# A graph network's convolution loops: sixteen additions on VectorE become one scan over feature-major blocks, with the turning done by ScalarE

## The reference

```python
def gcn_conv(x, edge_index, W, b, num_nodes):
    src = concatenate([edge_index[0], arange(num_nodes)])
    dst = concatenate([edge_index[1], arange(num_nodes)])
    deg = segment_sum(ones_like(dst), dst)
    dinv = where(deg > 0, rsqrt(deg), 0.0)
    norm = dinv[src] * dinv[dst]
    h = x @ W
    return segment_sum(h[src] * norm[:, None], dst) + b

h = relu(gcn_conv(x, edge_index, W1, b1, n))
out = relu(gcn_conv(h, edge_index, W2, b2, n))
```

## Time and profile before

| what | value |
|---|---|
| median of the runs | 10099.72 us |
| span of the profiled execution | 11181.7 us |
| first convolution, first gather to last addition | 3850.1 to 6042.5 us |
| second convolution, first gather to last addition | 6222.7 to 8414.6 us |
| GpSimd busy over the span | 7106.9 us (64%) |
| VectorE busy over the span | 4736.9 us (42%) |
| ScalarE busy over the span | 1142.1 us (10%) |
| TensorE busy over the span | 1801.6 us (16%) |

### The profile page before, as it was taken

The page is one execution under the profiler, slowest core; times in us unless marked ns, Lnnn a source line. Parts: engine busy times, 40 slices in busy tenths (PEclk is TensorE's granted clock), DMA queues, the critical chain, the costliest instruction groups (busy, mean ns, idle before and its releaser), DMA issues.

```text
span 11181.7 us, 57120 instructions
## 1 busy us (share of the span) xinstructions
PE 1801.6 (16%) x9285; PEld 1516.5 (14%) x9285; DVE 4736.9 (42%) x20005; ACT 1142.1 (10%) x2728; POOL 7106.9 (64%) x6884
## 2 busy tenths in 40 slices
PE   8744444444000400000000000000001000000000
PEld 7633333333000300000000000000000000000000
DVE  8855555555797422222221222222224344444446
ACT  0143434343000100000000000000000000000000
POOL 0566666666201377777776677777777776666766
PEclk7755555555555555555555555555555555555555
DMA  5144444444575111111111111111111222222221
GB/s 224 57 129 122 129 124 126 124 127 122 204 273 203 32 50 46 48 46 48 46 48 37 50 46 48 46 48 46 48 46 30 54 53 58 53 58 55 56 55 44
DMA packets 570444, 911.29 MB, mean 81 GB/s; under 512 B 333435, under 2 KB 348228, under 8 KB 544824
## 3 DMA queue, kind: packets, MB, share of 16 engines
q1 hardware_dynamic: 350264, 652.74, 17.3%
q0 software_dynamic: 219904, 255.88, 10.8%
HBM read 494.12 MB, written 414.02 MB: 81 GB/s over the span
## 4 chain that ended last, share of the span: by engine, by line
DVE 34%; issue 28%; another core or an unknown queue 17%; POOL 16%; PE 3%; DMA 1%; ACT 1%; DVEq 0%; SPq 0%; POOLq 0%; ACTq 0%
DVE arena_a L1495 16%; POOL arena_a L641 15%; DVE arena_b L1112 4%; DVE arena_a L1110 3%; DVE arena_b L1125 3%; DVE arena_a L1425 3%; POOL arena_a L610 2%; PE bank L811 2%; DVE arena_b L1056 1%; DVE arena_b L1093 1%; PE bank L916 1%; DVE arena_a L1625 0%; PE bank L890 0%; DMA arena_a<-in_a 0%
## 5 line engine op out<-in xcount | busy, mean ns | idle before, releaser
L641 POOL DMA_INDIRECT arena_a<-table_c,decay x3136 | 3284.6, 1047 | 1257.6 <-issue 1051.2
L1495 DVE SCALAR_TENSOR_TENSOR arena_a<-arena_a,same_dst 128x64 f32<-128x64 f32 x3134 | 891.5, 284 | 3449.5 <-DVE arena_a L1495 2713.2
L591 POOL DMA_INDIRECT by_src<-arena_b,idx_blk x1568 | 1570.8, 1002 | 885.8 <-issue 449.4
L641 POOL DMA_INDIRECT arena_a<-table_at,decay x1568 | 1556.8, 993 | 703.8 <-issue 468.4
L1110 DVE SCALAR_TENSOR_TENSOR arena_a<-arena_a,same_dst 128x64 f32<-128x64 f32 x1567 | 441.9, 282 | 711.1 <-remote 547.7
L864 PE MATMUL bank<-ident,chunk_end 128*64 128x128 f32 (+2 forms) x8 | 2.7, 442 | 4416.0 <-DVEq L973 4416.0
L864 PEld LDWEIGHTS bank<-ident,chunk_end 128*64 128x64 f32 (+2 forms) x8 | 1.4, 240 | 4416.6 <-DVEq L973 4416.6
L1112 DVE SCALAR_TENSOR_TENSOR arena_b<-arena_a,src_f,before 128x128 bf16<-128x128 f32 x1568 | 543.7, 347 | 37.4 <-issue 37.4
L850 PE MATMUL bank<-hrows 98*128 98x128 f32 x1568 | 404.0, 440 | 659.5 <-DVE arena_b L1125 331.9
L850 PE MATMUL bank<-hrows,arena_a 98*128 98x128 f32 x1568 | 403.3, 438 | 658.0 <-DVE arena_b L1125 347.4
L753 ACT ACTIVATE arena_b<-arena_a,decay 128x64 f32<-128x64 f32 x1568 | 394.2, 334 | 972.5 <-remote 610.2
(11 more groups left out here) (279 smaller groups left out, 4845.9 us busy)
## 6 DMA issues: line engine op xcount, KB each, us to landing
arena_a<-ids_rows SPq DMA_DIRECT2D x98, 1024.0 KB
states_src<-arena_a SPq DMA_DIRECT2D x98, 1024.0 KB
states_c<-arena_a SPq DMA_DIRECT2D x196, 512.0 KB
hrows<-by_src SPq DMA_DIRECT2D x98, 776.0 KB, 6.1
states_at<-arena_a SPq DMA_DIRECT2D x98, 576.0 KB
x_at_start<-arena_a SPq DMA_DIRECT2D x7, 7168.0 KB, 49.0
arena_a<-x_at_start SPq DMA_DIRECT2D x98, 512.0 KB
arena_a<-table_c,decay POOLq DMA_INDIRECT x3136
```

Source lines behind the costliest of these rows:

```text
L591: pool.indirect_dma_start(out=by_src, out_offset=AT(ap=idx_blk[r][:, k:k + 1], axis=0), in_=rows[r][:, k, :], in_offset=None)\
L641: pool.indirect_dma_start(out=gb[r][:, k * w:(k + 1) * w], out_offset=None, in_=table[g], in_offset=AT(ap=src_i[:, n * J + k:n * J + k + 1 ...
L1495: ins = v.scalar_tensor_tensor(out=st[h][:, k * D:(k + 1) * D], in0=old, scalar=same_dst[:, e:e + 1], in1=gb[r][:, k * D:(k + 1) * D], op0 ...
```

## The change

In the two convolutions (not in the attention) a block's sum is no longer sixteen additions. ScalarE copies the sixteen gathered rows of a block into a feature-major tile `in` of 64 x 17 (for each feature, a slot for the carried state and then the sixteen edges), and spreads the sixteen values of `same_dst` over a tile `mask` of the same form, whose first slots are zero. VectorE runs one `tensor_tensor_scan` over the 1088 flat elements (times mask, plus in) into a tile `sums`, and then copies the last slot of each feature into the first slot of the next `in`. ScalarE turns `sums` back to edge-major order into `st`, from where SyncE stores it as before. All four kinds of tiles are double. A gather buffer comes free when its rows are turned. On ScalarE, block n is turned before block n-1 is turned back.

```diff
-                    if n >= R:
+                    if n >= R and g == "at":
                         pool.wait_ge(s("state"), upto(g, "state") + n - R + 1)
+                    elif n >= R:
+                        pool.wait_ge(s("row_turned"), upto(g, "row_turned") + n - R + 1)
...
+        def mask_spread(act, g, n):
+            w = W3 if g == "at" else D
+            if n >= 2:
+                act.wait_ge(s("summed"), upto(g, "summed") + n - 1)
+            act.activation(features(f"mask{n % 2}", w)[:, :, 1:J + 1], bf(same_dst[:, n * J:(n + 1) * J], w), ACT.Copy)\
+               .then_inc(s("mask_spread"), 1)
+
+        def rows_back(act, g, n):
+            w, row = (W3, W3S) if g == "at" else (D, D)
+            act.wait_ge(s("summed"), upto(g, "summed") + n + 1)
+            if n >= 2:
+                act.wait_ge(s(f"stored{n % 2}"), upto(g, f"stored{n % 2}") + 16 * (n // 2))
+            act.activation(st[n % 2][:, 0:J * row].rearrange("p (j f) -> p j f", f=row)[:, :, 0:w],
+                           features(f"sums{n % 2}", w)[:, :, 1:J + 1].rearrange("p f j -> p j f"), ACT.Copy)\
+               .then_inc(s("state"), 1)
+
+        def conv_act(act, g):
+            act.wait_ge(s("masks_zeroed"), 1)
+            for n in range(NBLK):
+                r = n % R
+                mask_spread(act, g, n)
+                act.wait_ge(s(f"gathered{r}"), upto(g, f"gathered{r}") + (n // R + 1) * (16 * J))
+                act.activation(features(f"in{n % 2}", D)[:, :, 1:J + 1],
+                               gb[r][:, 0:J * D].rearrange("p (j f) -> p f j", f=D), ACT.Copy)\
+                   .then_inc(s("row_turned"), 1)
+                if n:
+                    rows_back(act, g, n - 1)
+            rows_back(act, g, NBLK - 1)
...
             def conv(g):
-                link(v.memset(chunk_end[:, :], 0.0))
-                chained = upto(g, "chain")
+                link(v.memset(features("in0", D)[:, :, 0], 0.0))
                 for n in range(NBLK):
-                    h, r = n % 2, n % R
+                    h = n % 2
                     if n >= 2:
-                        v.wait_ge(s(f"stored{h}"), upto(g, f"stored{h}") + 16 * (n // 2))
+                        v.wait_ge(s("state"), upto(g, "state") + n - 1)
                     if n:
-                        v.wait_ge(s("state"), upto(g, "state") + n)
-                    v.wait_ge(s(f"gathered{r}"), upto(g, f"gathered{r}") + (n // R + 1) * (16 * J))
-                    for k in range(J):
...
-                        ins = v.scalar_tensor_tensor(out=st[h][:, k * D:(k + 1) * D], in0=old,
-                                                     scalar=same_dst[:, e:e + 1],
-                                                     in1=gb[r][:, k * D:(k + 1) * D], op0=ALU.mult, op1=ALU.add)
...
+                        v.wait_ge(s("row_carried"), upto(g, "row_carried") + n)
+                    v.wait_ge(s("mask_spread"), upto(g, "mask_spread") + n + 1)
+                    v.wait_ge(s("row_turned"), upto(g, "row_turned") + n + 1)
+                    flat = slice(0, D * (J + 1))
+                    v.tensor_tensor_scan(by_feature[f"sums{h}"][:, flat], by_feature[f"mask{h}"][:, flat],
+                                         by_feature[f"in{h}"][:, flat], 0.0, ALU.mult, ALU.add).then_inc(s("summed"), 1)
+                    if n + 1 < NBLK:
+                        v.wait_ge(s("summed"), upto(g, "summed") + n + 1)
+                        v.tensor_copy(features(f"in{1 - h}", D)[:, :, 0], features(f"sums{h}", D)[:, :, J])\
+                            .then_inc(s("row_carried"), 1)
...
+            for h in range(2):
+                link(v.memset(by_feature[f"mask{h}"], 0.0))
+            tell("masks_zeroed")
             conv("c1")
```

## The result

The changed kernel takes 10435.65 us (median of 4 runs, 10432.88 to 10440.35). The kernel before, timed beside it, takes 10099.69 us (10092.31 to 10106.65). The ratio is 1.0334, 95% interval 1.0319 to 1.0349: 336 us slower, where 413 us were forecast.

A forecast was written before the change was run, and what follows sets the result against it. GpSimd issuing gathers was taken as the convolutions' bound. 10099.7 - 6 (additions) + 410 (gathers delayed by the scan) + 10 (carry copy) - 1 (tails) = 10513 us, 4.1% slower, range 10310 to 10600.

The forecast's parts named there:

- GpSimd is the bound, 19.99 us a block: Convolution loops: GpSimd issuing gathers sets the time, 16 x 1.2495 = 19.99 us a block; VectorE's work is covered.
- The slow pace of the traced execution is not in the runs: Convolutions: unprofiled blocks keep the trace's early pace; 1082 us between traced span and runs belong to the profiled execution.
- rival B: Convolutions: slow pace of 22.1 us a block is real unprofiled, the change removes it; 10064 or 9880 us; chance 0.07.
- The expected trace of 11145 us: Changed kernel's traced span: loops stay at 22.1 us a block, two tails shrink from 25.2 to about 7.3 us.
- Additions removed, -6 us: Convolution blocks: removing 16 hidden additions gains only 0.03 us a block, their cost to the gathers, 6 us in all.
- ScalarE, 1.09 us an operation: Convolution blocks: three new 1024-element operations, 3.3 us a block, covered; 2.2 us each if stepping doubled the price.
- A gather taken up inside the scan waits for its end and 0.8 us more: Convolution blocks: the scan stops a gather taken up during it, which ends about 0.8 us after the scan.
- Rival C: Convolutions: the scan does not hold the gathers up, or VectorE waits instead; no change, 10093 us; chance 0.05.
- The phase, 3.69 us after the sixteenth gather: Convolution blocks: scan starts there, catches the gather at 3.74, delays it 2.27 us, taken as 2.1; 410 us in all.
- rival A: Convolutions: slower turning puts the scan just past a gather's start; delay 1.2 us a block, 10327 us; chance 0.25.
- Carry copy, 10 us: After each scan: a 64-element copy of 0.21 us, taken as 0.05 a block, 10 us (0 to 41).
- Tails, -1 us: Ends of both convolutions: last gather to last sum falls from 7.6 to 7.3 us, -1 us for both.

The follow-up runs named there:

- again: The kernel before, unedited, run again on chip 4: 10096.2 us beside 10091.8, ratio 1.0002, traced span 10087.4.
- psum_mask: The changed kernel with the scan's mask input in PSUM: 10087.7 us, ratio 0.9995 on chip 4; repeated as psum_mask_b on chip 11: 11194.4 us, ratio 1.0006.
- plain_turn: The changed kernel with ScalarE reading the gathered numbers in order, not turning them (wrong sums): 10472.2 us, ratio 1.0378.
- short_scan: The changed kernel with a scan of 17 elements in place of 1088, other sums left out: 10086.8 us, ratio 0.9994.
- later768: The changed kernel with an extra 768-element ScalarE operation and a long-met wait between turning and scan, on chip 1: 11197.4 us, ratio 1.0012.

## Why the prediction came out as it did

**GpSimd is the bound, 19.99 us a block.** Held: 20.02 us in `again`, and the earlier trace rows show a normal block.

**The slow pace of the traced execution is not in the runs.** Right for the chip that was timed, with a wrong reason, so by luck. The prediction laid 1082 us to the one profiled execution, as if profiling or chance had made them. There are two paces among the chips used: on chip 4 the kernel before takes 10087 us in the trace and 10092 in the runs, on chips 1, 15 and 11 it takes 11181 to 11191 in unprofiled runs. The 11181.7 us of its first trace fit the second pace; which chip that trace came from is not on record. So rival B's premise was true somewhere, and its price wrong even there: it expected the change to take that pace away, and 1.0008 shows that it stays. The remark that VectorE became slow by itself and then disturbed GpSimd is not borne out either: in `psum_mask_b` the scan doesn't hold the gathers, and the pace remains. The expected trace of 11145 us was missed by the first trace of the change (10432.8), and came out at 11176.3 on chip 15. There the loops lasted as long as before, as it had said: 2167.9 us from the first to the last gather's start of c1, against 2167.2 in the first trace of the kernel before. The tails did shrink, from 26.4 to 9.3 us between the last gather's start and TensorE's first work, 17 us each. But what comes between that work and the next stage's first gather got longer, from 179.1 to 190.6 us after c1 and from 291.3 to 312.4 after c2. The reason for that is open.

**Additions removed, -6 us.** Their gathers were busy 2967.5 us in `again`, against 2960.4 for 3136 x 0.944: 7.1 us. It comes from the 250 gathers shown under `again`. So the prediction read its rows too coarsely where it said that the short additions don't stop a gather: a median of 944 and a longest of 980 ns leave room for holds of under 0.04 us, and those are there.

```profile
L641 POOL DMA_INDIRECT arena_a<-table_c,decay x3136 | 2967.5, 946 | 1039.9 <-issue 955.1
```

**ScalarE, 1.09 us an operation. This step failed.** Spreading took 1.04 us, but turning 1.94 and turning back 2.00: five us a block instead of 3.3. As an engine it stayed covered, as the bound of 2.2 us had it. But the length of the turning sets where the scan falls. The prices chosen for comparison, L703 and L681 of the kernel before with 64 elements, were too short to show the step. `plain_turn` shows it alone: the same 1024 elements in order take 1.06 us. The Trainium skill has a rule that would have warned: SBUF — State Buffer, in the part on the port swizzle under "SBUF: two separate sides", says that full bandwidth needs at least two accesses to the same line of 16 bytes. The turning reads a 4-byte number every 256 bytes. That its price doubled agrees; that the line is the cause was not tried.

**Scan, 2.47 us.** 2.425.

**A gather taken up inside the scan waits for its end and 0.8 us more.** Held, 0.75 to 0.76 us, where the scan's inputs are both in SBUF, but for gathers taken up in its first 0.05 us (`plain_turn`). It is what `short_scan` and `psum_mask` take away: 10435.7 becomes 10086.8 and 10087.7. Rival C is out.

**The phase, 3.69 us after the sixteenth gather, and a delay of 2.27, taken as 2.1.** The scan came at 4.56, past the point, as in rival A: the gather of +3.74 escaped and the one of +4.99 was caught. The point was misplaced as well: the prediction let a gather be caught that had started up to 0.12 us before the scan (its 3.86 against 3.74), and so had 2.45 us as the largest delay; the longest one measured is 2.19, with the gather 0.05 us behind the scan's start. And both delays were mis-sized. With the scan at s us after the sixteenth gather's start, the next gather to start at t and the scan's end at s+2.42, the delay is s+2.42+0.76-t-0.94. For the change that is 4.56+2.24-4.99 = 1.81. For `plain_turn` (s is 5023.94-5020.32 = 3.62) it is 3.62+2.24-3.74 = 2.12, for `later768` 0.97 us ahead of its gather 2.24-0.97 = 1.27; both were read in the traces. Rival A's 1.2 us took a scan that starts just past the point as if it stayed there; with a turning of 1.94 us it is 0.82 us past it, and the delay has grown back to 1.8. The time fell between forecast and rival A for that reason: A's mechanism, at nearly the forecast's price. That it lies nearer to the forecast than to A's 10327 us is luck of the turning's length. This term, taken as 410 us and measured as 342, is also most of the difference in the number.

**Carry copy, 10 us.** Nothing: the held gather ends 0.76 us after the scan in any case (5033.42), 0.49 after the copy. The copy lies in that gap, so its own effect can't be read there. `short_scan` lets it be read. The two gathers that had 0.17 us of the copy before them ended 0.82 us after it, as beside an addition, which suggests that the copy holds a gather too; but it is so short that this costs at most 0.04 us. The 31 us that the prediction worked out for this case took the copy's whole 0.21 us in every block, and did not appear.

**Tails, -1 us.** From the last gather's start to the first work of TensorE after c1 it is 5600.61-5591.22 = 9.4 us; two stepped operations of 2 us lie in it in a row with the scan. In `again` it was 5428.89-5420.92 = 8.0. So +1.4 each, 2.8 for both.

**Sums of the prediction.** One doesn't come out: 10064 less 196 x 0.9 is 9888, not 9880. It is a price of rival B and changes nothing.

**The sum with measured terms:** 10099.7-7.1+341.6+2.8 = 10437.0 us, measured 10435.65. The difference from the forecast of 10513 is the delay (342 instead of 410), the copy (0 instead of 10), and the tails.

## What to carry to other kernels

Beside indirect DMAs that GpSimd issues without slack, don't count VectorE's busy time: count the longest single operation with two SBUF inputs and where it falls among the gathers. What a gather pays here is what is left of that operation when it is taken up, less some 0.2 us (0.94-0.76). Sixteen short ones (4.5 us in all) cost 0.04 us a block, one of 2.4 us cost 1.7, the same one with an input in PSUM cost nothing. And before an old trace is used, hold its span against the runs: if they differ by 10%, ask whether it came from another chip before giving the difference to the profiler.

## What was not expected of the hardware

- One input of the scan in PSUM frees GpSimd fully: the longest of 3136 gathers took 1050 ns.
- A gather is held only by what is left of the VectorE operation beyond 0.13 us (additions) or 0.19 us (scan), and not at all if it is taken up within 0.044 us of the scan's start.
- A faster ScalarE made the kernel slower (1.06 against 1.94 us of turning, 10472 against 10436, ratios 1.0378 and 1.0334), since it moved the scan against GpSimd's rhythm.
- Two paces of the same kernel: 10092 us on chip 4, 11181 to 11191 on chips 1, 15 and 11. Each of these chips was used at one time only, so what belongs to the chip and what to the time can't be told apart. In a stage whose code is a loop of the program, VectorE does the same work in the same time at both paces; at 1000 to 2000 us, in unrolled code, it gets less done at the slower one. The windows' columns are PE, PEld, DVE, ACT and POOL busy. First the trace of before, then `again`:

```profile
2900.00:3400.00 500.00, 0.00 (x0) 0.00 (x0) 494.36 (x2665) 0.00 (x0) 0.00 (x0) 0.50 0.77 273
1000.00:2000.00 1000.00, 429.30 (x1989) 372.39 (x1988) 578.25 (x3485) 409.24 (x908) 662.14 (x661) 0.50 0.43 126
```

```profile
2600.00:3100.00 500.00, 0.00 (x0) 0.00 (x0) 494.34 (x2666) 0.00 (x0) 0.00 (x0) 0.50 0.77 273
1000.00:2000.00 1000.00, 492.05 (x2288) 428.37 (x2288) 631.92 (x4001) 467.81 (x1039) 767.18 (x764) 0.50 0.49 145
```

In the loop VectorE does 2665 and 2666 instructions, in the unrolled code 3485 and 4001. A slow supply of instructions in long unrolled code would fit this, but no run here varied it, so the cause stays open.
